# A four-layer mixer and expert network: column-ordered queries, tables made one stage earlier, expert results scattered chunk by chunk

## Time and profile before

| | us |
|---|---|
| median of three runs | 810.92 (805.61 to 813.16) |
| profiled execution | 812.87 |
| span of the profiled execution | 811.2 |
| PE busy | 668.7 (82%), weight loads 556.4 |
| DVE busy | 387.0 (48%) |
| ACT busy | 303.1 (37%) |
| POOL busy | 229.2 (28%) |
| mean granted TensorE clock | 0.889 |

### The profile page before, as it was taken

One profiled execution on the slowest core, in us unless ns is written; L12 is line 12 of the kernel. 1 busy time (PEld: TensorE's weight loads), 2 busy tenths in 40 slices (PEclk: granted clock), 3 DMA queues, 4 the chain that ended last, 5 costly groups with the idle time before them and its releaser, 6 DMA issues. The chain is left out here.

```text
span 811.2 us, 12856 instructions
## 1 busy us (share of the span) xinstructions
PE 668.7 (82%) x4034; PEld 556.4 (69%) x4034; DVE 387.0 (48%) x978; ACT 303.1 (37%) x604; POOL 229.2 (28%) x274
## 2 busy tenths in 40 slices
PE   4888936997996999957989983799995798898397
PEld 2476725685794899953677763699994367776296
DVE  4566816114445433314578756343440466885301
ACT  2344524232413344422434552235442243454222
POOL 5176620001200044442045400724334204541000
PEclk9989977798996899985899995899998589999599
DMA  3745720634206166533497503577653349840442
GB/s 90 195 114 142 176 57 0 156 99 96 48 1 175 40 161 160 121 48 65 131 248 212 111 17 113 149 177 183 170 124 48 70 132 233 222 114 1 102 119 72
DMA packets 92485, 95.14 MB, mean 117 GB/s; under 512 B 17313, under 2 KB 78644, under 8 KB 92424
## 3 DMA queue, kind: packets, MB, share of 16 engines
q1 hardware_dynamic: 78952, 74.91, 34.6%
q0 software_dynamic: 11808, 18.38, 11.3%
q10 hardware_dynamic: 1680, 1.28, 0.6%
HBM read 66.92 MB, written 27.84 MB: 117 GB/s over the span
## 5 line engine op out<-in xcount | busy, mean ns | idle before, releaser
L2017 POOL DMA_INDIRECT sum_scratch<-area,f_row_index x48 | 72.4, 1509 | 177.6 <-DVE area L1963 167.9
L881 DVE TENSOR_REDUCE neg_max<-psum 128x4 f32<-128x1024 f32 x72 | 87.9, 1221 | 31.0 <-PE psum L767 30.2
L1722 PE MATMUL psum<-w,area 128*112 128x192 f32 (+1 forms) x576 | 96.2, 326 | 0.0
L1722 PEld LDWEIGHTS psum<-w,area 128*112 128x112 f32 (+1 forms) x576 | 93.5, 183 | 0.0
L961 POOL TENSOR_TENSOR shift<-ident,neg_max 128x256 fp32r<-128x256 f32 x96 | 66.5, 704 | 84.8 <-DVE neg_max L881 56.4
L779 PE MATMUL psum<-q_parts,k_parts 128*128 128x256 f32 x288 | 78.5, 303 | 0.4
L780 PE MATMUL psum<-shift,ones_r 128*128 128x256 f32 x288 | 74.2, 289 | 0.0
L767 PE MATMUL psum<-k_parts,q_parts 128*128 128x256 f32 x288 | 52.9, 307 | 19.9 <-DVE neg_max L881 8.6
L1821 DVE TENSOR_TENSOR q_parts<-w,q_parts 128x1536 fp32r<-128x1536 f32 x16 | 28.1, 1758 | 82.7 <-ACT q_parts L1751 82.7
L779 PEld LDWEIGHTS psum<-q_parts,k_parts 128*128 128x128 f32 x288 | 56.7, 197 | 10.8 <-issue 8.2
L360 PE MATMUL psum<-ident,x_norm 128*96 128x128 f32 x128 | 26.1, 349 | 45.0 <-DVE x_norm L330 44.8
(11 more groups left out here) (250 smaller groups left out, 1328.9 us busy)
## 6 DMA issues: line engine op xcount, KB each, us to landing
w<-in_f_w_dram SPq DMA_DIRECT2D x32, 576.0 KB, 4.8
w<-in_f_w_dram SPq DMA_DIRECT2D x16, 384.0 KB, 4.4
w<-in_f_w_dram SPq DMA_DIRECT2D x32, 192.0 KB, 5.2
q_parts<-q_scratch SPq DMA_DIRECT2D x32, 192.0 KB, 3.6
q_scratch<-area SPq DMA_DIRECT2D x22, 192.0 KB, 2.1
k_parts<-k_scratch SPq DMA_DIRECT2D x63, 64.0 KB, 3.1
q_parts<-q_scratch SPq DMA_DIRECT2D x32, 96.0 KB, 2.9
q_parts<-q_scratch SPq DMA_DIRECT2D x40, 64.0 KB, 3.3
```

Of the source, the lines that this page charges most:

```text
L881: ins = dve.tensor_reduce(most, ps[:, 0:2, :].rearrange("p b (c k) -> p (b c) k", c=2), AX_X, ALU.max, negate=True)
L1722: ins = pe.matmul(ps[0:R, 6 + c // 2, D * (c % 2):D * (c % 2 + 1)], x.hidden[:, fc, R * c:R * (c + 1)], net.w2[:, b, fc, :], start=(fc == ...
L2017: pool.indirect_dma_start(net.sum_dram[:, :], bass.IndirectOffsetOnAxis(ap=row_index[0:size, b, c:c + 1], axis=0), x.y[0:size, b, c, :], N ...
```

## The change

It has four edits.

1. The queries get a second, column-ordered copy `query_by_column`, in a part of `w2` that holds the keys later. DVE makes it in four copies, one behind each `q_sb`, where its two table multiplications stood. PE waits for all four ahead of the width products and reads them from there, 16 neighbours at a time.
2. The tables are made in the preceding mixture block: PE makes them behind its last expert and ahead of the norm (`table_products`, bank 2), DVE spreads them behind its last results and ahead of the norm (`table_of_heads`). The prologue no longer has them, nor the wait for them.
3. The three chunks of an expert's result go to bank 6, bank 7 and the second half of bank 6. PE counts `y_ps` up after each chunk, DVE takes each chunk by itself and counts `y_sb` up three times an expert, POOL waits for each chunk by itself.
4. Since chunk 2 is written to the bank from which DVE reads chunk 0, PE waits ahead of chunk 2 until `y_sb` says that chunk 0 of the same expert is done.

The core of the diff:

```diff
+        self.query_by_column = w2[:, 0:2 * TOK].rearrange("p (h b a) -> p h b a", h=2, b=SIDE)
...
     def project_tensor(pe):
-        if not m.local:
-            for n in range(2):
-                pe.matmul(ps[0:HC, 6 + n, 0:IMG_TOK], m.rel_rows[:, n, :], net.rel_pick[:, :],
-                          start=True, stop=True).then_inc(table_ps, 1)
...
             pe.wait_ge(q_sb, 4)
-            pe.wait_ge(table_sb, 2)
             for kind in range(2):
+                if kind == 1:
+                    pe.wait_ge(q_by_column, 4)
...
-                        q = query[:, :, pos, :] if kind == 0 else query[:, :, :, pos]
+                        q = query[:, :, pos, :] if kind == 0 else parts.query_by_column[:, :, pos, :]
...
-            for n in range(2):
-                dve.wait_ge(table_ps, n + 1)
...
+            for b in range(4):
+                half, tc = b // 2, b % 2
+                dve.wait_ge(q_sb, b + 1)
+                dve.tensor_copy(parts.query_by_column[:, half, :, rows * tc:rows * (tc + 1)],
+                                parts.query[:, half, 512 * tc:512 * (tc + 1)].rearrange("p (a b) -> p b a", b=SIDE)
+                                ).then_inc(q_by_column, 1)
...
+def table_products(net, m, pe, table_ps):
+    for n in range(2):
+        ins = pe.matmul(net.psum[0:HC, 2, IMG_TOK * n:IMG_TOK * (n + 1)], m.rel_rows[:, n, :], net.rel_pick[:, :], start=True, stop=True)
+    ins.then_inc(table_ps, 1)
...
+def table_of_heads(net, dve, table_ps):
+    dve.wait_ge(table_ps, 1)
+    for n in range(2):
+        each = [HC, IMG_TOK, HALF_HEADS]
+        dve.tensor_tensor(net.rel[:, n, :, :].rearrange("p a (b j) -> p (a b) j", j=HALF_HEADS),
+                          net.psum[0:HC, 2, IMG_TOK * n:IMG_TOK * (n + 1)].rearrange("p (m u) -> p m u", u=1).to_broadcast(each),
+                          net.head_mask[:, :].rearrange("p (u j) -> p u j", u=1).to_broadcast(each), ALU.mult)
...
+    def products_of(c, size):
+        return ps[0:size, 6 + c % 2, D * (c // 2):D * (c // 2 + 1)]
...
-                pe.wait_ge(y_sb, START + 2 * n)
+                pe.wait_ge(y_sb, START + CHUNKS * n)
                 pe.wait_ge(w2_loaded[b], pair(r, e, b) * (W2_LOADS * DMA) + W2_LOADS * DMA)
                 for c in range(CHUNKS):
+                    if c == 2:
+                        pe.wait_ge(y_sb, START + CHUNKS * n + 1)
                     for fc in range(FCH):
                         if c == 0:
                             pe.wait_ge(hidden_sb, HIDDEN_BANKS + n * FCH + (fc + 1))
-                        ins = pe.matmul(ps[0:R, 6 + c // 2, D * (c % 2):D * (c % 2 + 1)], x.hidden[:, fc, R * c:R * (c + 1)],
+                        ins = pe.matmul(products_of(c, R), x.hidden[:, fc, R * c:R * (c + 1)],
                                         net.w2[:, b, fc, :], start=(fc == 0), stop=(fc == FCH - 1))
-                    if c > 0:
-                        ins.then_inc(y_ps, 1)
+                    ins.then_inc(y_ps, 1)
...
             each_round(pe, one_round)
+            table_products(net, following, pe, table_ps)
             norm.tensor(pe)
...
-                for bank, chunks in ((6, 2), (7, CHUNKS - 2)):
...
+                for c, size in enumerate(sizes):
+                    dve.wait_ge(y_ps, START + CHUNKS * job(r, e) + (c + 1))
+                    y, src = x.y[0:size, b, c, :], products_of(c, size)
                     if with_bias:
...
+                        dve.tensor_tensor(y, src, net.b2[0:size, b, :], ALU.add).then_inc(bias_added, 1)
+                        dve.wait_ge(bias_added, CHUNKS * job(r, e) + (c + 1))
+                        src = y
+                    dve.tensor_scalar(y, src, row_weight[0:size, b, c:c + 1], None, ALU.mult).then_inc(y_sb, 1)
...
             each_round(dve, one_round)
+            table_of_heads(net, dve, table_ps)
             norm.vector(dve, reloaded)
...
                 for c, size in enumerate(sizes):
-                    if c != 1:
-                        pool.wait_ge(y_sb, START + 2 * job(r, e) + (2 if c else 1))
-                        pool.sem_inc(round_begun, 1)
+                    pool.wait_ge(y_sb, START + CHUNKS * job(r, e) + (c + 1))
+                    pool.sem_inc(round_begun, 1)
```

More of the change, by code:

```diff
@@ L489, in attention @@
     qk_ps, q_sb, k_sb = (sem(f"{tag}_{n}") for n in ("qk_psum", "q_sbuf", "k_sbuf"))
+    q_by_column = sem(tag + "_q_by_column")
     v_ps, v_sb = sem(tag + "_v_psum"), sem(tag + "_v_sbuf")
-    table_ps, table_sb = sem(tag + "_table_psum"), sem(tag + "_table_sbuf")
     rel_ps, rel_h_sb, rel_w_sb = (sem(f"{tag}_{n}") for n in ("rel_psum", "rel_h_sbuf", "rel_w_sbuf"))
@@ L645, in project_vector @@
         if not m.local:
-            for n in range(2):
-                dve.wait_ge(table_ps, n + 1)
[L648 to L652, removed]
+            rows = 512 // SIDE
+            for b in range(4):
[4 more added lines that the diff above has]
+                                ).then_inc(q_by_column, 1)
         take_low(dve, 0, 2)
@@ L1471, in __init__, with moe_feed_forward @@
         self.spread = cut(P, 2 * E_MOE * CAPACITY).rearrange("p (b e c) -> p b e c", b=2, e=E_MOE)
-def moe_feed_forward(net, tag, slots, capacity, gate, norm):
+def table_products(net, m, pe, table_ps):
[9 more added lines that the diff above has]
+                          net.head_mask[:, :].rearrange("p (u j) -> p u j", u=1).to_broadcast(each), ALU.mult)
+def moe_feed_forward(net, tag, slots, capacity, gate, norm, following):
     nc, ps, d = net.nc, net.psum, net.dram
@@ L1552, in moe_feed_forward @@
     sum_begun = sem(tag + "_sum_begun")
+    table_ps = sem(tag + "_table_psum")
     slots_marked, slots_used = sem(tag + "_slots_marked"), sem(tag + "_slots_used")
@@ L1612, in one_round @@
             def one_round(r):
-                sp.wait_ge(y_sb, START + 2 * job(r, 0))
+                sp.wait_ge(y_sb, START + CHUNKS * job(r, 0))
                 for e in range(2):
@@ L1629, in one_round @@
                             load_rows(e, b)
-                        sp.wait_ge(y_sb, START + 2 * job(r, e) - 2)
+                        sp.wait_ge(y_sb, START + CHUNKS * job(r, e) - CHUNKS)
                         load_w2(e, b)
@@ L1951, in results @@
                 dve.wait_ge(added, BEFORE + job(r, e) - 1)
-                for bank, chunks in ((6, 2), (7, CHUNKS - 2)):
[L1953 to L1956, removed]
-                    if with_bias:
[L1958 to L1964, removed]
+                for c, size in enumerate(sizes):
+                    dve.wait_ge(y_ps, START + CHUNKS * job(r, e) + (c + 1))
+                    y, src = x.y[0:size, b, c, :], products_of(c, size)
+                    if with_bias:
+                        dve.tensor_tensor(y, src, net.b2[0:size, b, :], ALU.add).then_inc(bias_added, 1)
+                        dve.wait_ge(bias_added, CHUNKS * job(r, e) + (c + 1))
+                        src = y
+                    dve.tensor_scalar(y, src, row_weight[0:size, b, c:c + 1], None, ALU.mult).then_inc(y_sb, 1)
             def one_round(r):
@@ L2057, in metaformer @@
         norm = Norm(net, 4)
-        moe_feed_forward(net, "f1", SLOTS_CAPPED, CAPACITY, gate, norm)
+        moe_feed_forward(net, "f1", SLOTS_CAPPED, CAPACITY, gate, norm, l2)
         net.recycle_semaphores()
@@ L2064, in metaformer @@
         norm = Norm(net, 6)
-        moe_feed_forward(net, "f2", SLOTS_MAX, None, gate, norm)
+        moe_feed_forward(net, "f2", SLOTS_MAX, None, gate, norm, l3)
         net.recycle_semaphores()
```

## The result

| | before, us | after, us |
|---|---|---|
| median of the runs | 811.5 (805.61 to 813.16, four) | 824.7 (823.68 to 828.32, four) |
| profiled execution | 812.87 | 823.68 |
| its span | 811.2 | 822.0 |
| mean granted TensorE clock | 0.889 | 0.895 |

The two profiled executions differ by 10.8, the medians by 13.2, the ratio says 17.1 (0.0211 x 811.5), 14.1 to 20.1 by its interval. The gap between these is mostly on the side of before: its profiled execution was one of its longer ones, and 21 further runs of it had a median of 808.0. So terms are compared with terms in the traces, and whole kernels by their ratios.

The account below looks back on a forecast made before the run. PE was taken as gapless in the mixtures, a chain as bounding the borders; 812.87 + 23.0 - 4.3 - 3.8 - 4.2 = 823.6 profiled, less 1.95 to the median: 821.7, rounded 822, range 819 to 829.

Parts of the forecast that it names:

- The wait ahead of chunk 2: Second products in f1 and f2: PE stands until DVE has done chunk 0, 13 stalls of 1.65 to 1.94, +23.0.
- The release: From DVE finishing chunk 0 to PE starting chunk 2, first weight load included: taken as 0.15.
- Chunk by chunk: Ends of f1 and f2: earlier scatters gain 2.0 and 2.3, sum -4.3; nothing gained inside an expert.
- The tables: Heads of the prologues: table products leave, queries start 1.99 earlier, worth 1.9 each, twice: -3.8.
- the cover: Before the norm: idle PE and DVE hide the moved table work, 1.7 to spare; without it up to 5.4 each.
- The copy: Prologues: width products read column-ordered queries at the faster pace, 3.3 less on PE, 2.1 at the end, twice: -4.2.
- From there low part, copy, low part, copy, copy: DVE's chain in the prologue after ACT's cast: 4.2 with overlaps, last copy at 396.8 instead of 398.57, gain 1.8.
- what is late next is DVE, not PE: Prologue after the copy's gain: keys, stores, their reload and the first maximum hang on DVE; no separate size.
- The rival of the falling clock: Mixtures: stalls bring PE's clock down, +21 after each stall or +11 after every second; 832 to 843, chance 0.13.
- DVE did not meet the wait: No-stall rival, second products: DVE has chunk 0 done by 3.90, only gains stay; 800.6, or 798.6 against the median; 0.10.
- Gain and loss did not cancel: Rival: prologues win 5.6 more than summed, stalls as priced; 816, range 803 to 819, chance 0.15.
- The useless copy: Prologues: slow width pace is not from the step, 4.2 missing; 826, within the forecast's 0.62 chance.

Follow-up runs that it names:

- the filling: 14 unread f32 matmuls behind the value products of l2 and l3, added to the reordered changed kernel (802.83, ratio 0.9906): 799.88, ratio 0.9873.
- the step sweep: Changed kernel plus five sets of eight matmuls behind f1's tables, moving-operand steps 1, 2, 4, 8 and 16; ran once, 827.24.
- the filled kernel: Changed kernel, DVE's chunk 0 before the split (f2's expert 0: expert 1's weights split first), plus the filling: 799.88, ratio 0.9873.
- the fastest kernel: The filled kernel, but f2's expert 0 has its third chunk in its own bank, unwaited, and DVE's old order: 797.35, ratio 0.9842.

## Why the prediction was right

The direction and the mechanism came out, and the time lies in the range of 819 to 829: 822 was forecast, 824.7 is the median. The sum was +10.7, and the two profiled executions differ by 10.8, but that it is met to a tenth is luck. The stretches that the change touches differ by 14.9, and 4.1 of that is taken off by stretches that it does not touch, where before's profiled execution was long. By the ratios the change costs 17.1 (14.1 to 20.1), more than was forecast: edits 1 and 2 gained 3.8 (2.5 to 5.1) where 8.0 was forecast, edits 3 and 4 cost 21.1 (18.5 to 23.8) where 18.7 was.

- **The wait ahead of chunk 2: right.** +23.0 forecast, +24.0 in the table (12.11 + 11.92). It fell on seven experts of f1 (third chunk at 5.46 to 5.56) and six of f2 (5.67 to 5.75). The release was 0.05 and not 0.15, so the delays of these thirteen add up to 22.4 and not 23.0. Two things were missing: expert 0 of f2 stalls as well, 0.44, because its rows are loaded late, and each expert loses some 0.09 more than its third chunk is late (12.11 / 7 = 1.73 for a delay of 1.64). Taking the wait out of f1 gave back 11.4, and taking DVE's chunk 0 ahead of its split ended the stalls with the wait in place. So it is shown that the loss lies in the position of the result in DVE's list, not in the number of waits or scatters.
- **Chunk by chunk: right.** From PE's last product record to the reload 6.92 became 4.84 in f1 (-2.08) and 7.94 became 5.69 in f2 (-2.25), for a forecast of 2.0 and 2.3. These are trace readings; no experiment has this edit alone. In l3 0.49 of it is given back: from the norm's first input to the block's start it is 10.17 instead of 9.68, in every kernel with this edit. The cause of that is open.
- **The tables: right.** 3.8 forecast, 4.4 by the kernel with the tables put back, with an uncertainty of about 3; the cover was there (2.51 to spare, 1.7 forecast). The traces show that 1.92 goes from the head of each prologue, but also that the time from the first query product to the first relative product varies from 9.6, where the clock rose 3.6 behind the first query product, to 11.3, where it rose 7.0 behind it. In l3 it was 10.38 before and 11.29 after, so 0.9 of the tables' gain is missing there.
- **The copy: the term was mis-sized.** The step, "From there low part, copy, low part, copy, copy", held in the prologue: the time from the first relative product to DVE's first keys fell from 14.14 to 11.95 (-2.19, forecast 2.1) in both layers, and on PE the relative products took 7.23 instead of 10.69 (-3.46, forecast 3.3). But 4.2 was booked for the end of the kernel, and by the runs the copy alone is worth 1.1 with an uncertainty of about 3. That "what is late next is DVE, not PE" came out as well; what the sum put at nothing is what PE's idle time then costs. PE stood 3.71 for the loads of the keys, which come behind DVE's work, the clock was at 0.50 behind that, and the first six maxima took up to 0.97 longer. That this lengthening goes with the clock is shown by the 28 layers of the 14 kernels, and by the first score records, 1.19 without the filling and 0.71 with it. With PE kept busy in the gap, copy and filling together were worth about 5. That the clock is all that the copy's gain was lost to is not shown.
- **The rival of the falling clock: refuted for this change.** The clock was 1.00 in both mixtures with an idle time of 1.4 to 1.7 in every expert that waits, and its mechanism is real at twice that: with 3.44 the window stood at 0.84. It also acted where I had not looked, ahead of the first scores. The Trainium skill, page "TensorE: Matmul & The Clock Gate", section "A second HAM failure mode: psum-queue depth-cycling", says that frequent short idles between groups of matmuls make the clock swing. At the idles of this change the trace does not agree, at 3.44 it does.
- **The other rivals.** DVE did not meet the wait, since its first result came 5.08 behind the start. Gain and loss did not cancel. The useless copy would have been 826, nearer to the median than the forecast; but its reason, that the pace is not from the step, is refuted by the step sweep. The copy did change the pace, and the gain was lost later.

**What stays open.** The kernel with edits 1 and 2 alone won 3.8 by its runs. In its trace the stretches from the last product record to the first maximum are 7.95 shorter, as forecast, and the first six maxima 1.57 longer, which leaves 6.4. Some of the missing 2.6 may be before's profiled execution being long in these stretches too, but this was not isolated. And it is not shown why the filling kept the clock at 1.00 in l3 of one kernel and not in its l2, nor in either layer of the fastest kernel, where the first six maxima took 11.69 and 11.82.

## What to carry to other kernels

A wait for another engine costs what stands ahead of the awaited instruction in that engine's list, so before a PSUM bank is shared one reads that list and moves the result forward; here moving two calls ahead of two others turned 2.1% slower into 0.6% faster. A saving in front of a transfer lasts only as far as the next thing that arrives late, and if TensorE then stands idle it may restart at half its clock. A term taken from the profile of one execution carries that execution's own luck, here several microseconds, and is checked with ratios.

## What the runs showed of the hardware

- The pace of float32 records depends on the step of the moving operand with one jump: 0.109 and 0.113 us at steps of 1 and 2 elements, 0.218 to 0.233 at 4, 8 and 16.
- An idle time of 1.4 to 1.7 us in every 12 to 14 left the granted clock at 1.00; one of 3.44 in every 15 to 17 brought it to 0.84 over 80 us, and made the records behind it take 7.15 where they had taken 4.06. The length of one idle time does not decide alone: in l2 of the filled kernel the clock fell to 0.50 behind 2.30 us of which PE was busy 0.98, and in its f2 behind one idle time of 2.88.
- With the granted clock at 1.00 throughout, the stretch from the first to the sixth maximum took 10.98 to 11.00 us in seven layers; with a stretch at 0.50 in it, 11.48 to 12.40 in 21.
- From the end of DVE's multiplication to the start of the PE record that waited for it took 0.05 us in every stalled expert, where it was 0.80 from DVE to POOL's scatter. Whether that is the engine or the kind of instruction was not tested.
